# Turning the attention rows of heads 2 and 3 on VectorE and DMA as well, and dealing the products over the gaps between scores

## What is computed

```python
x = x + _L2_xattn_ref(_layernorm(x), ctx, ...)   # "attention 3"
x = x + _L2_ffn_ref(_layernorm(x), ...)
x = x + _L3_xattn_ref(_layernorm(x), ctx, ctx, ...)   # "attention 4"
x = x + _L3_ffn_ref(_layernorm(x), ...)
```

```python
scores = jnp.einsum('bqhd,bkhd->bhqk', q * SCALE, k)
attn = jax.nn.softmax(scores, axis=-1)
out = jnp.einsum('bhqk,bkhd->bqhd', attn, v)   # then out @ w_out
```

## The kernel before

| tile | TensorE behind scores | VectorE behind the maximum | ScalarE behind the exponentials |
|---|---|---|---|
| 0 | prep place 0 | low_out(st-2, 0) | high_out(st-2, 1), place 0 |
| 1 | place 1 | place 0 | place 1 |
| 2 | transposes 2 | low_out(st-2, 1), place 1 | copy 2 |
| 3 | transposes 3 | copy 3 | |
| 4 | | | |
| 5 | project(st-2), transposes 4, place 2 | add_up(st-2), turn head 0 | copy 4, place 2 |
| 6 | place 3 | turn head 1, place 2 | place 3 |
| 7 | values(st-1, 0 and 1), rest | place 3 | high_out(st-1, 0) |

## Time and profile before

### The profile page before, as it was taken

One profiled execution on the slowest core, in us unless ns is written; L12 is line 12 of the kernel. 1 busy time (PEld: TensorE's weight loads), 2 busy tenths in 40 slices (PEclk: granted clock), 3 DMA queues, 4 the chain that ended last, 5 costly groups with the idle time before them and its releaser, 6 DMA issues.

```text
span 1211.9 us, 21865 instructions
## 1 busy us (share of the span) xinstructions
PE 1035.8 (85%) x6575; PEld 782.6 (65%) x6575; DVE 724.8 (60%) x2474; ACT 627.3 (52%) x2087; POOL 572.2 (47%) x926
## 2 busy tenths in 40 slices
PE   4988899869889988979999997676789999987995
PEld 3875788835556667856667665566566676654994
DVE  5565264476776772387877775322877777852444
ACT  2344323347778714358777763223387777731221
POOL 5223665452000142657555656366375556665552
PEclk9987999978999989979999997788889999987997
DMA  3003556599700124023223311354342223214676
GB/s 64 13 27 98 174 165 208 168 157 358 267 2 1 35 63 142 35 88 118 75 88 105 115 45 44 89 177 133 88 122 89 88 71 105 71 34 129 203 208 174
DMA packets 157284, 134.30 MB, mean 111 GB/s; under 512 B 20907, under 2 KB 131171, under 8 KB 157168
## 3 DMA queue, kind: packets, MB, share of 16 engines
q1 hardware_dynamic: 146560, 114.18, 31.8%
q0 software_dynamic: 8448, 17.20, 4.3%
q10 hardware_dynamic: 2160, 1.53, 0.5%
...
## 4 chain that ended last, share of the span: by engine, by line
PE 62%; DVE 15%; issue 7%; ACT 6%; DMA 3%; POOL 3%; another core or an unknown queue 2%; SPq 1%; ACTq 0%; DVEq 0%; POOLq 0%
PE ps L2829 5%; PE ps L2921 4%; PE ps L3043 4%; PE ps L2934 4%; PE ps L2831 4%; PE ps L2830 4%; PE ps L3025 3%; PE ps L3571 3%; PE ps L3575 3%; PE ps L3224 2%; ACT ex L1365 2%; PE ps L3057 2%; PE ps L3584 2%; DVE ln_st L1770 2%
## 5 line engine op out<-in xcount | busy, mean ns | idle before, releaser
L1365 ACT ACTIVATE ex<-ps,nmx 128x154 f32<-128x154 f32 x512 | 194.3, 391 | 83.7 <-DVE nmx L2320 82.3
L1127 POOL TENSOR_TENSOR pp<-ex,rc 128x256 f32<-128x256 f32 x256 | 157.6, 616 | 143.7 <-DVE rc L2325 143.0
L2320 DVE TENSOR_REDUCE nmx<-ps 128x2 f32<-128x308 f32 x256 | 118.1, 463 | 49.9 <-PE ps L2831 48.9
L2829 PE MATMUL ps<-kp,q_s 128*128 128x308 f32 x256 | 99.5, 389 | 25.2 <-ACT ex L1365 22.8
L964 POOL DMA_INDIRECT yq_d<-yq,ids_q x78 | 74.7, 957 | 78.2 <-DVE yq L2072 58.7
L1365 ACT ACTIVATION_READ_ACCUMULATOR ex<-ps,nmx 128x1 f32 x512 | 104.7, 205 | 0.0
L1482 ACT ACTIVATE pe<-ps,nmx 128x154 f32<-128x154 f32 x256 | 84.9, 394 | 31.9 <-DVE nmx L2203 30.8
L2829 PEld LDWEIGHTS ps<-kp,q_s 128*128 128x128 f32 x256 | 51.1, 200 | 57.5 <-ACT ex L1365 30.9
L934 POOL TENSOR_TENSOR ln_r<-ln_v,mhalf 128x4 f32<-128x4 f32 x32 | 32.7, 1021 | 103.5 <-DVE ln_v L1778 86.1
L2830 PE MATMUL ps<-kp,q_s 128*128 128x308 f32 x256 | 81.5, 318 | 0.0
L2831 PE MATMUL ps<-kp,q_s 128*128 128x308 f32 x256 | 81.2, 317 | 0.0
...
...
## 6 DMA issues: line engine op xcount, KB each, us to landing
...
```

The costliest lines, as they stand in the source:

```text
L1127: pool.tensor_tensor(pp[st % 2][:, m % 4, 2 * j:2 * j + 2, :], w[:, :, 0:P], r.broadcast_to([P, 2, P]), ALU.mult)
L1365: ins = act.activation(ex[:, tt % NEX, j, :], ps[:, tt % 3, j * SK:(j + 1) * SK], ACT.Exp, bias=nmx8[:, tt % 8, j:j + 1], accum_out=sm8[:, ...
L2320: dve.tensor_reduce(nmx8[:, tt % 8, :], ps[:, tt % 3, 0:2 * SK].rearrange("p (h s) -> p h s", h=2), AX.X, ALU.max, negate=True).then_inc(n ...
L2829: mm(bank, w[0], x[0], start=first, stop=False)
```

## The change

Heads 2 and 3 go the same way as heads 0 and 1, as a second set with semaphores of its own: `pt_b`, `pt_d` and the landing place (now `pt_all`) hold four heads, VectorE turns c = 2 and 3 of the step before behind maxima 2 and 3, and SyncE serves both sets in turn. This is so for steps 0 to 13 (set 0: 0 to 14). TensorE's transposes 2 and 3 and their copies fall away there; c = 4 stays. `values(st, 1)` and `rest_values(st)` come a step and a half after their scores instead of at the end of the next step. The work between the scores is placed anew; `SPOT` moves preps 2 and 3 to places 11 and 12:

| tile | TensorE behind scores | VectorE behind the maximum | ScalarE behind the exponentials |
|---|---|---|---|
| 0 | places 0 and 1 | place 0 | place 0 |
| 1 | place 2 | place 1 | place 1 |
| 2 | values(st-2, 1) | turn head 2 (st-1), place 2 | place 2 |
| 3 | rest_values(st-2) | turn head 3 (st-1) | |
| 4 | transposes 4 (st-1) | low_out(st-2, 0) | high_out(st-2, 0) |
| 5 | place 3 | turn head 0, low_out(st-2, 1) | high_out(st-2, 1), copy 4 |
| 6 | values(st-1, 0) | turn head 1, place 3 | place 3 |
| 7 | project(st-2) | add_up(st-2) | |

In prep 12 (here and in attention 2) the loops over batches and heads are exchanged. The diff, cut to its core:

```diff
@@ -71,7 +71,7 @@
     NST = B * 4
     PREPS = 13
     PRIOR = (None, None, 7, 8)
-    SPOT = (0, 2, 3, 4, 5, 6, 7, 8, 9, 10, 11, 12, 13)
+    SPOT = {0: 0, 2: 1, 3: 4, 4: 5, 5: 6, 6: 7, 7: 8, 8: 9, 9: 10, 10: 11, 11: 2, 12: 3, 13: 12}
 
 
     ORDER = [(g, b) for g in range(2) for b in range(B)] + [(2, 0), (2, 1), (3, 0), (3, 1), (2, 2), (3, 2), (2, 3), (3, 3)]
@@ -81,11 +81,11 @@
     FIRST1 = {1: [0], 2: [1], 3: [2, 3]}
     BEHIND1 = {(14, "D"): [("u", 0)], (15, "A"): [("f", 0)], (15, "D"): [("u", 1)]}
     TAIL = [("f", 1), ("t", 0), ("pt", NST - 1, 3), ("o", NST - 2), ("pt", NST - 1, 1), ("pt", NST - 1, 2), ("u", 2), ("pt", NST - 1, 4), ("f", 2), ("t", 1), ("t", 2), ("o", NST - 1), ("u", 3), ("f", 3), ("t", 3)]
-    LAST_TURNED = NST - 2
+    LAST_TURNED = (NST - 2, NST - 3)
 
     def by_blocks(st, c):
 
-        return c < 2 and 0 <= st <= LAST_TURNED
+        return c < 4 and 0 <= st <= LAST_TURNED[c // 2]
 
     NEXT = [("next", 0, i) for i in range(PREPS)]
     ENDING = [None, None] + [[("pt", NST - 1, 1), ("rk", 0), ("pt", NST - 1, 4), ("pt", NST - 1, 3), ("f", 2), ("lg", 1), ("y", NST - 2), ("pt", NST - 1, 2), ("rk", 1), ("t", 2), ("y", NST - 1), ("lg", 2), ("f", 3)]
...
@@ -106,9 +106,8 @@
                 return [] if by_blocks(x, c) else [("pt", x, c)]
 
             late, later = 0 < st, 2 <= st
-            names += turned(st - 1, 1) * late + spot(0) + spot(1) + behind("A") + [("pt", st - 1, 2)] * late
-            names += [("pt", st - 1, 3)] * late + [("y", st - 2)] * later + [("pt", st - 1, 4)] * late + spot(2) + behind("C")
-            names += spot(3) + behind("D") + turned(st, 0)
+            names += spot(0) + spot(1) + spot(2) + behind("A") + behind("C") + turned(st - 1, 2) * late
+            names += [("pt", st - 1, 4)] * late + spot(3) + turned(st - 1, 3) * late + [("y", st - 2)] * later + behind("D") + turned(st, 0)
         names += ENDING[l]
         place = {name: r for r, name in enumerate(names)}
         by_act = [name[0] in ("t", "x") or name[0] == "pt" and name[2] in (0, 2, 4) for name in names]
...
@@ -339,8 +338,8 @@
         w_room = sb("w_room", [P, 4, 4 * P])
         w1_s = [over(f"w1_s{u}", [P, 4 * P], F32, w1_at + 2048 * u)[0] for u in range(2)]
         w2_s = [over(f"w2_s{u}", [P, 4, D], F32, w1_at + 4096 + 2048 * u)[0] for u in range(2)]
-        pt_b = over("pt_b", [P, 2, S], F32, w1_at)[0]
-        pt_pair = over("pt_pair", [P, 2, S], F32, pt_at)[0]
+        pt_b = over("pt_b", [P, 4, S], F32, w1_at)[0]
+        pt_all = over("pt_all", [P, 4, S], F32, pt_at)[0]
 
         x_hi, x_lo = q_s[:, 0, :], q_s[:, 1, :]
 
...
@@ -735,17 +738,23 @@
 
             def blocks_home(l, between):
 
-                for st in range(LAST_TURNED + 1):
+                def brought(st, j):
+
                     if st or l > 2:
-                        sp.wait_ge(*moved_blocks(l, st - 1))
-                    for c in range(2):
+                        sp.wait_ge(*moved_blocks(l, st - 1, j))
+                    for c in (2 * j, 2 * j + 1):
                         sp.wait_ge(*turned_blocks(l, st, c))
-                        sp.dma_start(pt_d[c * P:(c + 1) * P, :], pt_b[:, c, :]).then_inc(n_wrote, 16)
-                    sp.wait_ge(*wrote_blocks(l, st))
-                    wait(sp, n_va, sides(l) + 2 * st - 1)
+                        sp.dma_start(pt_d[c * P:(c + 1) * P, :], pt_b[:, c, :]).then_inc(n_wrote[j], 16)
+                    sp.wait_ge(*wrote_blocks(l, st, j))
+                    wait(sp, n_va, sides(l) + 2 * st - 1 + j)
                     for o in range(4):
-                        sp.dma_start(pt_pair[32 * o:32 * o + 32, :, :].rearrange("k c (a q) -> k (c a) q", q=P),
-                                     pt_d[:, o * P:(o + 1) * P].rearrange("(a k) q -> k a q", k=32)).then_inc(n_moved, 16)
+                        sp.dma_start(pt_all[32 * o:32 * o + 32, 2 * j:2 * j + 2, :].rearrange("k c (a q) -> k (c a) q", q=P),
+                                     pt_d[2 * j * P:(2 * j + 2) * P, o * P:(o + 1) * P].rearrange("(a k) q -> k a q", k=32)).then_inc(n_moved[j], 16)
+
+                for st in range(NST):
+                    for j in range(2):
+                        if by_blocks(st, 2 * j):
+                            brought(st, j)
                     if st in between:
                         raw_weights(*between[st])
 
...
@@ -1402,29 +1411,30 @@
                 turned_x(0)
                 for st in range(NST):
                     exps(st, 0)
-                    high_out(st - 2, 1)
                     step_prep(st, 0)
                     exps(st, 1)
                     step_prep(st, 1)
+                    exps(st, 2)
+                    step_prep(st, 2)
+                    exps(st, 3)
                     if st == 0:
                         turned_x(1)
+                        turned_x(2)
                     elif st == 2:
                         turned_x(3)
-                    exps(st, 2)
+                    exps(st, 4)
+                    high_out(st - 2, 0)
+                    exps(st, 5)
+                    high_out(st - 2, 1)
                     copy_pt(st - 1, 2)
-                    exps(st, 3)
-                    exps(st, 4)
-                    exps(st, 5)
                     copy_pt(st - 1, 4)
-                    step_prep(st, 2)
-                    if st == 0:
-                        turned_x(2)
                     exps(st, 6)
+                    step_prep(st, 3)
                     if st == 15:
                         scale(l, 1)
-                    step_prep(st, 3)
                     exps(st, 7)
-                    high_out(st - 1, 0)
+                    if st == NST - 1:
+                        high_out(st - 1, 0)
                     if st >= 14:
                         tail_xT(l, st - 14)
                     copy_pt(st, 0)
...
@@ -2335,10 +2345,10 @@
                 def turn_blocks(st, c):
 
                     if by_blocks(st, c):
-                        dve.wait_ge(n_z, base(l - 1, 8 * NST) + 8 * st + 4)
+                        dve.wait_ge(n_z, base(l - 1, 8 * NST) + 8 * st + (4 if c < 2 else 8))
                         if st or l > 2:
-                            dve.wait_ge(*wrote_blocks(l, st - 1))
-                        dve.transpose(pt_b[:, c, :], pp[st % 2][:, :, c, :].rearrange("p t (o k) -> p o t k", o=4)).then_inc(n_turn, 1)
+                            dve.wait_ge(*wrote_blocks(l, st - 1, c // 2))
+                        dve.transpose(pt_b[:, c, :], pp[st % 2][:, :, c, :].rearrange("p t (o k) -> p o t k", o=4)).then_inc(n_turn[c // 2], 1)
 
                 def low_out(st, j):
 
...
@@ -2416,47 +2426,49 @@
                 measured(2)
                 for st in range(NST):
                     maxima(st, 0)
-                    low_out(st - 2, 0)
-                    copy_pt(st - 1, 1)
-                    if st == 1:
-                        variances(3)
-                    maxima(st, 1)
                     step_prep(st, 0)
                     if st == 0:
                         normed_half(2, 0)
-                    maxima(st, 2)
-                    low_out(st - 2, 1)
+                    elif st == 1:
+                        variances(3)
+                    maxima(st, 1)
                     step_prep(st, 1)
                     if st == 0:
                         normed_half(2, 1)
-                    elif st in (13, 14):
-                        tail_sum(l, st - 13)
-                    elif st == 15:
-                        tail_shift(l, 1)
-                        best(l, 0)
+                    maxima(st, 2)
+                    turn_blocks(st - 1, 2)
+                    step_prep(st, 2)
                     maxima(st, 3)
-                    copy_pt(st - 1, 3)
-                    if st == 14:
-                        tail_scale(l, 0)
-                    elif st == 15:
-                        indices(l, 0)
-                    maxima(st, 4)
+                    turn_blocks(st - 1, 3)
                     if st == 0:
                         summed_up(3)
                     elif st == 1:
                         normed_half(3, 0)
-                    maxima(st, 5)
-                    add_up(st - 2)
+                    maxima(st, 4)
+                    low_out(st - 2, 0)
                     if st == 0:
                         moments_half(3, 0)
                     elif st == 1:
                         normed_half(3, 1)
                     elif l == 2 and st == 5:
                         item_limits()
+                    elif st in (13, 14):
+                        tail_sum(l, st - 13)
+                    elif st == 15:
+                        tail_shift(l, 1)
+                        best(l, 0)
+                    maxima(st, 5)
                     turn_blocks(st, 0)
+                    low_out(st - 2, 1)
+                    if st == 14:
+                        tail_scale(l, 0)
+                    elif st == 15:
+                        indices(l, 0)
```

(40 more changed lines are left out.)

32 lines of the change are left out of this document (17 added, 15 removed).

## The result

| | before | after |
|---|---|---|
| median of four runs each, us | 1212.12 | 1302.32 (1294.15 to 1306.6) |
| ratio, 95% interval | | 1.0728 [1.0647, 1.0808] |
| profiled execution, its span, us | 1213.6, 1211.9 | 1306.2, 1304.4 |
| mean granted TensorE clock | 0.922 | 0.897 |

What follows compares the result with a forecast made beforehand. TensorE was taken to bound the kernel, VectorE close behind; with waits on VectorE, steps 4 to 11 +37.6, 1 to 3 +2.4, 12 to 14 +7.6, the rest 0, summed to +47.6: 1258 us, range 1226 to 1284.

Steps and rivals of the forecast that it cites:

- Trips: VectorE's maximum, ScalarE's exponentials and copy, then VectorE's subtraction: 2.11 us for a tile with a prep, against 0.86 without waiting.
- `low_out` waiting: VectorE's `low_out` behind maxima 4 and 5 waits for ScalarE's `high_out`, by 1.3 and 0.6 us.
- steps 9: Attention steps 5 and 9, with four preps: VectorE's chain counted at 15.5 us.
- step 10: Attention steps 6 and 10, where the fourth prep is a plain copy of VectorE: counted at 15.1 us.
- nearly all of 32: VectorE's kp subtractions wait for ScalarE's copy in nearly all of 32 cases, by about 1.2 us.
- SyncE's queue: Two sets a step, about 10 us, hide behind the steps; as a rival it sets the pace, 1220 us, chance 0.06.
- Half clock: Rival: TensorE, idling in the 12 long steps, pays +1.6 us in each, +19, 1277 us in all; chance 0.12.
- Steps 7 and 11: Attention steps whose preps are plain copies alone: counted at 11.3 us each.
- Steps 0 and 15: First and last steps of each attention loop: put at 0, in one term with the stages outside.
- steps 1 to 3: Steps without preps early in each attention: 33.0 against 31.8 us, +1.2, or +2.4 in both attentions.
- 12 to 14: Late attention steps with the tail's work on VectorE: taken as 38 us, +3.8, or +7.6 in both attentions.
- Outside the loops: Stages outside the attention loops: 0, between -2 and +4 together with steps 0 and 15.

Runs made afterwards that it cites:

- late_all: Changed kernel with VectorE's `step_prep` and `low_out` both moved behind the next maximum; ratio to before 1.0208.
- late_outs: Changed kernel with only VectorE's two `low_out` moved behind the next maximum, its preps left in place; ratio to before 1.035.
- old_early_preps: Kernel before the change, with VectorE's `step_prep` moved behind the maximum of its own tile; ratio to before 1.0231, some 28 us.
- filled: Changed kernel with idle products on TensorE where it waits, so that its clock stays up; ratio to before 1.0562, steps 4 to 11 248.9 us in both attentions.
- the 15.15 us step above: Step 8 of attention 4, at full clock, in the changed kernel with prep 1 moved from behind scores 1 to behind scores 5; that kernel's ratio 1.0586.

## Why the prediction was wrong in size

**What held.** *The mechanism and its price.* Trips of 2.10 us (2.11 counted), `low_out` waiting 1.34 and 0.72 (1.3 and 0.6), steps 9 of 15.44 (15.5), step 10 of 14.98 in attention 3 (15.1; 16.03 in attention 4, at a clock of 0.89), TensorE idle 21% of step 9 of attention 4 (a quarter), next to no wait for `pt_all`. late_all, late_outs and old_early_preps show it as a cause from both sides. One detail was off: all 32 kp subtractions wait, but 1.16 us only at places 0 and 1; at 2 and 3 a turn ahead covers half (0.55), which the count had and the sentence on "nearly all of 32" had not. *The sign*, and that SyncE's queue doesn't matter here: two sets fill some 11 us (from reads to reads 5.60 and 5.83 us in step 12 of attention 4), and the steps last 11.4 to 20.8 but for step 1.

**What failed.** The excess over the count is 92.5 - 47.6 = 45 us, in five terms.

*Half clock was left out of the sum* and stood as a rival of 0.12. It had been priced from one row of four at +1.6 a step, "+19". Measured: 11.0 us in steps 4 to 11 (259.9 against 248.9 in filled), 15 in both loops, and in the median 1.0728 against 1.0562, which is about 20 us, though in two batches and with intervals that overlap. So the price of 19 for the long steps was too high by the traces, and the chance of 0.12 far too low: TensorE's idle time in the steps with preps rose from between 0 and 2 us to between 2.2 and 5.2, and of the sixteen steps with preps twelve had a clock under 1.00, where before it was one. In after, step 8 goes so (TensorE's row, then VectorE's):

```profile
1037.06 0.45 PE L2841 MATMUL ps<-wqT,wkT 128*128 128x128 f32 x1 [2.81 <-DVE wkT L1895]
...
1039.44 0.41 PE L2843 MATMUL ps<-wqT,wkT 128*128 128x128 f32 x1
```

```profile
1040.78 0.48 DVE L2330 TENSOR_REDUCE nmx<-ps 128x2 f32<-128x308 f32 x1 [3.15 <-PE ps L2843]
```

The twelve matmuls of prep 1 take 2.6 us instead of the 1.37 of the earlier trace rows, at 1.2 instead of 2.4 GHz, behind a wait of 2.81, and VectorE's next maximum waits for them. Here the half clock lies on the chain. The Trainium skill, "TensorE: Matmul & The Clock Gate", on the HAM clock gate, which the prediction cited, says that the clock is set by how busy the engine has been lately. These rows agree; the 15.15 us step above, which idled 3.5 us in all at 1.00, shows that idle time made the loss likely, not certain.

*Steps 7 and 11, counted 11.3, took 13.1 to 14.1 (13.5 at full clock): +9 over four.* The count had "plain copies alone" on VectorE and forgot TensorE: preps 3 and 12 both stand ahead of scores 1, and `project`, `add_up` and the next step's maximum 0 follow each other with `low_out` late. In step 7 of attention 4 of after VectorE waits for TensorE 0.51 us in front of maximum 1 (the first row), 0.47 in front of maximum 4 and 1.54 in front of `add_up` (the second), 2.5 of the 2.8 us over the count; in filled, at full clock, it is 0.51, 0.47 and 0.98, 2.0 of 2.2:

```profile
1021.00 0.48 DVE L2330 TENSOR_REDUCE nmx<-ps 128x2 f32<-128x308 f32 x1 [0.51 <-PE ps L2843]
...
1032.80 0.69 DVE L2371 TENSOR_TENSOR acc<-acc,ps 128x512 f32<-128x512 f32 x1 [1.54 <-PE ps L2843]
```

*`item_limits`: +3.1.* 19 small operations of VectorE in step 5 of attention 3, in no row of the prediction. Before, VectorE's slack had all but covered them. Now they stand in its chain:

```profile
609.27 0.14 DVE L1996 CAST bits<-row_no 128x1 int32<-128x1 f32 x1
...
611.61 0.48 DVE L2330 TENSOR_REDUCE nmx<-ps 128x2 f32<-128x308 f32 x1
```

That is 2.34 us between `low_out` and the next maximum, and step 5 took 18.54 us where steps 9 took 15.44 (18.40 in filled). What the other 0.8 us are I haven't split. These two terms are nearly all of the 12.1 us by which filled's 248.9 exceeds the counted 236.8.

*The edges of the loop: +14.5.* Steps 0 and 15 were put at 0 and took 5.7 more, steps 1 to 3 +4.1 and 12 to 14 +4.7 over their terms; some 4 of this is half clock again (15 - 11). In these steps work of the neighbouring stages runs on VectorE, which the count took as covered. That each of its operations counts once VectorE is the chain would explain the rest, but no run moves this work alone, so it isn't shown.

*Outside the loops: +7.7, put at -2 to +4.* The larger part, 6.4, lies between the two attentions, in the experts' stage, which the change doesn't touch; its stretches there have a lower clock than before (0.82 against 0.90 in the last). Of the seventeen kernels sixteen took 2.4 to 6.5 us more than before between the loops, old_early_preps (+3.5), which has nothing of the change there, among them, and spread 0.8 less; so the change as such isn't shown to be the cause. Those kernels ran on chips where before itself took 4 to 13 us more than here, which may be the same thing. What the cause is stays open.

So the step that failed was the sum: it took the steps at the edges and the stages outside at 0, `item_limits` not at all, steps 7 and 11 by VectorE alone and the clock as before, although its own finding was that the pace moves to another engine. Each of these errors has the same sign, and the range, made of rivals with one mechanism each, didn't hold their sum.
